# A transformer layer on one core: P times V in pairs, and the last transposes of P grouped with the first pair

## What is computed

```python
xn, ln = _ln(x, g_x, b_x), _ln(latents, g_l, b_l)
q = ln @ w_q
k, v = jnp.split(jnp.concatenate([xn, ln], axis=1) @ w_kv, 2, axis=-1)
sim = jnp.einsum('bhid,bhjd->bhij', q * scale, k)      # 64 x 576 a head
attn = jax.nn.softmax(sim, axis=-1)
out = jnp.einsum('bhij,bhjd->bhid', attn, v)
return _ln(out @ w_out, g_o, b_o)
```

## Time and profile before

| | before |
|---|---|
| profiled execution, us | 987.43 |
| its span, us | 985.6 |
| TensorE busy | 956.3 us, 97% |
| VectorE busy | 769.4 us, 78% |
| ScalarE busy | 440.2 us, 45% |
| GpSimd busy | 130.7 us, 13% |
| granted clock of TensorE | 1.00 |
| P times V, 1280 matmuls | 43.1 + 21.4 us |

### The profile page before, as it was taken

How to read it: one execution, slowest core, us unless ns; L and a number is a source line. 1 busy time by engine, 2 the same in 40 slices (tenths; PEclk the granted TensorE clock), 3 DMA queues, 4 the chain that set the end, 5 groups by cost and what they waited for, 6 DMA issues and landing times.

```text
span 985.6 us, 16666 instructions
## 1 busy us (share of the span) xinstructions
PE 956.3 (97%) x6400; PEld 778.0 (79%) x6400; DVE 769.4 (78%) x1647; ACT 440.2 (45%) x848; POOL 130.7 (13%) x145
## 2 busy tenths in 40 slices
PE   8999999999999999999999999999999999999997
PEld 7778788787888787887878888777676778888885
DVE  6547588789788888887887884578888598999985
ACT  4533664565366456546545653723333322222221
POOL 6420000101110101100111010023122000000000
PEclk9999999999999999999999999999999999999999
DMA  6688565866877684767758466081002950000000
GB/s 216 186 273 206 183 105 159 190 88 191 156 130 154 150 175 110 188 150 138 129 145 197 80 181 174 5 213 34 1 2 76 264 131 12 11 11 12 12 12 22
DMA packets 119451, 120.06 MB, mean 122 GB/s; under 512 B 47430, under 2 KB 88070, under 8 KB 117324
## 3 DMA queue, kind: packets, MB, share of 16 engines
q1 hardware_dynamic: 111980, 93.30, 35.5%
q0 software_dynamic: 6816, 24.64, 14.3%
q10 hardware_dynamic: 576, 1.05, 0.3%
HBM read 89.04 MB, written 29.93 MB: 121 GB/s over the span
## 4 chain that ended last, share of the span: by engine, by line
PE 53%; DVE 17%; DMA 12%; issue 7%; ACT 5%; SPq 4%; POOL 1%; DVEq 0%; ACTq 0%
PE ps_banks L147 13%; PE ps_banks L149 12%; PE ps_banks L148 12%; DMA scratch_rstd<-sb_rstd_b 7%; PE ps_banks L472 4%; SPq L132 4%; PE ps_banks L679 3%; DVE sb_kfull L915 2%; DVE sb_kT_lo L886 2%; PE ps_banks L746 2%; PE ps_banks L747 2%; PE ps_banks L748 2%; PE ps_banks L598 2%; DVE sb_b_stats L847 2%; DMA scratch_mean<-sb_a_mean_row 1%
## 5 line engine op out<-in xcount | busy, mean ns | idle before, releaser
L1442 ACT ACTIVATE sb_kT_hi<-sb_kfull 128x512 fp32r<-128x512 f32 x64 | 40.5, 632 | 161.2 <-DVE sb_kfull L915 161.2
L147 PE MATMUL ps_banks<-sb_zT_hi,sb_wkv_hi 128*128 128x512 f32 x256 | 106.1, 414 | 0.1
L149 PE MATMUL ps_banks<-sb_zT_hi,sb_wkv_lo 128*128 128x512 f32 x256 | 100.4, 392 | 0.0
L148 PE MATMUL ps_banks<-sb_wkv_lo,sb_zT_hi 128*128 128x512 f32 x256 | 100.3, 392 | 0.0
L147 PE MATMUL ps_banks<-sb_wkv_hi,sb_zT_hi 128*128 128x512 f32 x256 | 100.1, 391 | 0.0
L149 PE MATMUL ps_banks<-sb_wkv_hi,sb_zT_lo 128*128 128x512 f32 x256 | 100.0, 391 | 0.0
L148 PE MATMUL ps_banks<-sb_zT_lo,sb_wkv_hi 128*128 128x512 f32 x256 | 99.9, 390 | 0.0
L966 DVE CUSTOM_DVE_ANT_0 sb_probs<-ps_banks,sb_maskbias 128x576 f32<-128x576 f32 x64 | 48.1, 751 | 35.9 <-PE ps_banks L149 35.5
L147 PE MATMUL ps_banks<-sb_wgu,sb_z_hi 128*128 128x512 f32 (+1 forms) x192 | 73.7, 384 | 0.0
L148 PE MATMUL ps_banks<-sb_wgu,sb_z_hi 128*128 128x512 f32 (+1 forms) x192 | 72.1, 375 | 0.0
L149 PE MATMUL ps_banks<-sb_wgu,sb_z_lo 128*128 128x512 f32 (+1 forms) x192 | 71.9, 375 | 0.0
(11 more groups left out here) (268 smaller groups left out, 2419.0 us busy)
## 6 DMA issues: line engine op xcount, KB each, us to landing
sb_ctx<-in_ctx SPq DMA_DIRECT2D x16, 1024.0 KB
sb_ctxT<-in_ctx_t SPq DMA_DIRECT2D x16, 1024.0 KB, 8.3
scratch_wgu<-sb_w_both POOLq DMA_DIRECT2D x22, 512.0 KB
sb_wgu<-scratch_wgu SPq DMA_DIRECT2D x44, 256.0 KB, 4.7
sb_wdn<-scratch_wdn SPq DMA_DIRECT2D x8, 704.0 KB, 7.8
scratch_q<-sb_a_qk POOLq DMA_DIRECT2D x8, 512.0 KB, 6.2
sb_rstd_row<-scratch_rstd SPq DMA_DIRECT2D x16, 256.0 KB, 4.9
sb_qpack<-scratch_q SPq DMA_DIRECT2D x32, 128.0 KB, 8.5
```

The source lines that it names most:

```text
L147: e.matmul(o, wh, xh, start=i == 0, stop=False)
L148: e.matmul(o, wh, xl, start=False, stop=False)
L149: m = e.matmul(o, wl, xh, start=False, stop=i == n - 1)
L1442: e.activation(dst, src, ACT.Identity).then_inc(done)
```

## The change

TensorE: in the slots 0 to 3 P is now touched at two places. Slot 0 has K0 alone. Slot 1 turns P2 and P3, does P times V of the pairs 0 and 1, and then both lone transposes of P2 and P3, side by side in one bank; slot 3 does the pairs 2 and 3. In slots 6 and 7 nothing moves. ScalarE's copies follow, with one read-out signal for the two lone ones. The split of the last quarter of w_out moves from the end of batch 0 and slot 0 of batch 1 to slots 2 and 3 of batch 1.

```diff
             def transpose_p(b, n):
...
-                bank = claim(("pt", b, n))
-                e.transpose(psum[0:LQ, bank, 0:P], probs[j][:, chunk(b, CS)], ident[:, :]).then_inc(filled[bank])
+
+            def transpose_p_latents(b, *tiles):
+                bank = claim(("pt", b, tiles[0]))
+                for j, n in enumerate(tiles):
+                    took["pt", b, n] = took["pt", b, tiles[0]]
+                    on.wait_ge(p_normed, C * b + n + 1)
+                    m = e.transpose(psum[0:LQ, bank, j * P:(j + 1) * P], probs[n % 2][:, chunk(b, CS)], ident[:, :])
+                m.then_inc(filled[bank])
...
-                    if old and slot < 4:
-                        weigh_v(b - 1, slot)
-                    if old and slot < 2:
-                        transpose_p(b - 1, slot + 2)
+                    if old and slot == 1:
+                        transpose_p(b - 1, 2)
+                        transpose_p(b - 1, 3)
+                        weigh_v(b - 1, 0)
+                        weigh_v(b - 1, 1)
+                        transpose_p_latents(b - 1, 2, 3)
+                    if old and slot == 3:
+                        weigh_v(b - 1, 2)
+                        weigh_v(b - 1, 3)
                     if cur and slot >= 6:
                         transpose_p(b, slot - 6)
+                        transpose_p_latents(b, slot - 6)
...
-                    if b == 1 and slot == 0:
+                    if b == 1 and slot == 3:
                         lo_of_w_out(C - 1)
...
-                bank = taken(("pt", b, n))
-                copy(p_t[j][0:LQ, CS, :], psum[0:LQ, bank, 0:P], drained[bank])
+
+            def copy_p_latents(b, *tiles):
+                bank = taken(("pt", b, tiles[0]))
+                for j, n in enumerate(tiles):
+                    if C * b + n >= 2:
+                        on.wait_ge(v_weighed, C * b + n - 1)
+                    m = e.activation(p_t[n % 2][0:LQ, CS, :], psum[0:LQ, bank, j * P:(j + 1) * P], ACT.Copy)
+                m.then_inc(drained[bank])
...
-                    if old and slot < 2:
-                        copy_p(b - 1, slot + 2)
+                    if old and slot == 1:
+                        copy_p(b - 1, 2)
+                        copy_p(b - 1, 3)
+                        copy_p_latents(b - 1, 2, 3)
                     if cur and slot >= 6:
                         copy_p(b, slot - 6)
+                        copy_p_latents(b, slot - 6)
...
-                    if b == 0 and slot >= 4:
+                    if b == 0 and 4 <= slot < 7:
                         hi_of_w_out(slot - 4)
+                    if b == 1 and slot == 2:
+                        hi_of_w_out(C - 1)
```

## The result

The changed kernel took 1004.56 us (median of four runs, 999.98 to 1006.07) where the kernel before took 987.24 on the same chip (four runs, 984.4 to 989.51): ratio 1.0152, 95% interval 1.0128 to 1.0176. The forecast was 996, 985 to 1002. It went the way that was forecast, and nearly twice as far, so that it ended 2.6 us above the range.

A forecast was written before the change was run, and what follows sets the result against it. TensorE, 97% busy, was taken to just keep up with a loop through rstd's memory round trip. Odd batches +6.8, batch 1 +1.3, even +2.8, last -0.3 made 10.6; about 1.5 back left +9: 996 us, range 985 to 1002.

The forecast's parts named there:

- The mechanism: K1 waits for K0's own bank in even batches, for the turned weight's in odd batches 3 to 13; +9 us.
- the gain taken back: About 1.5 us subtracted from the sum, where an earlier K0 or a turn read out earlier helps.
- the last batch: Term of the sum for the final batch: -0.3 us.
- the wait for V: On TensorE, the first P times V no longer waits for the copy of V: 3.7 us saved.
- that for `tile_lo`: TensorE's later wait, up to 1.1 us, shrinks by what the scores came later.
- Laps to `sb_b_ve`: From K0 scaled to VectorE's last statistics: odd batches with a turn +6.8 us in all, even ones +2.8, batch 1 +1.3.
- The trip: Round trip of rstd through memory, from VectorE's last statistics to the next K0 scaled: still 18 to 19 us.
- What TensorE saves: Grouped P times V saves 0.6 us a batch, 9 to 10 over 15; with the V wait, 13 to 14 us.
- The first rival: TensorE's queue is the bound after all; if banks are free in time, 14 us come off: 973 us; chance 13%.
- The bound on the turn's bank: How much earlier the turned weight's bank is free with ScalarE's half in a shorter queue: 0 to 1.1 us, odd batches.
- It decides if K0 is scaled within 2.6 us of its end: Condition for the rival that TensorE's queue bounds the kernel: VectorE scales K0 before TensorE needs the bank for K1.
- The rule of the Trainium skill: Independent matmul groups should rotate through different PSUM banks; by it alone the change is a loss, with no number given.

The follow-up runs named there:

- the changed kernel again: The unaltered changed kernel run once more on the chip of the other experiments, as yardstick: ratio 1.0061 to the kernel before on the same chip.
- the freest order: Against the kernel before: P2 turned ahead of K0, P3 behind the first pair, both pairs, lone transposes behind K1; 0.9986, or 0.9937 with K scaled by a row always in SBUF.
- the kernel before without the row wait: The kernel before with K scaled by g_o, a row always in SBUF, so nothing waits for rstd's landing: ratio 0.9990 to the kernel before.
- the row always there: The changed kernel with K scaled by a row always in SBUF, spill and load of rstd kept: ratio 0.9987 to the kernel before.
- the kernel with y scaled later: The changed kernel with VectorE's two operations on y_row moved behind the scaling of K1 in odd batches: ratio 1.0210 to the kernel before.
- the first pair: The kernel before and the changed kernel as first measured, on one chip: 987.24 and 1004.56 us, ratio 1.0152.

## Why the prediction was half right

*The mechanism held, the size did not.* The steps that failed are terms of the sum: the gain taken back, the last batch, batch 0 and the clock at nothing. K1 starts 0.05 behind the weight's read-out in odd batches and 0.06 behind K0's scaling in even ones; the wait for V and that for `tile_lo` are gone, P times V is 4.3 us shorter (15 x 0.3 = 4.5 forecast). From K0 scaled to the first scores an even batch takes 10.3 (forecast 10.3) and an odd one with a turn, but for batch 3 with its dip of the clock, 11.55 to 11.8 (forecast 1.70 + 0.05 + 9.8). Laps to `sb_b_ve` grew by 7.4 in the odd batches without the dip of the clock (forecast 6.8, written for 6 x 1.1 = 6.6), 2.0 in the even ones (2.8), 1.7 in batch 1 (1.3): 11.1 for 10.9. The trip stayed at 18.5.

*What was mis-sized* is the rest of the sum, 9 forecast and 16.5 found:
- "I take about 1.5 back" did not come: 1.5. Every such gain lies inside the trip, which didn't shorten.
- the last batch, -0.3, was +1.0: 1.3. In turn 16 the transposes of P3 wait for its last scaling; some of it is the clock, at 0.91 in 640 to 660; the changed kernel again has the same wait of 3.0 there and 0.91 in 620 to 640.
- batch 0, +1.0, not foreseen; whether it is the moved w_out is not settled.
- the clock: 1.6 in batch 3, and 1.8 behind turn 16, of which the dip in the last stage is 1.6, in no term of mine. The first follows on a stand of TensorE of 1.7 us, which the new wait made; that it caused the dip is not shown, and nearly the same stand in the batches 7 and 9 had none behind it. The last can't be tied to the change: from its first matmul with `sb_wdn` to the end a kernel takes 177.2 to 177.3 us in 15 of the 20 profiles, the changed kernel again among them, and 178.8 in five.
The laps were 0.2 more. 0.2 + 1.5 + 1.3 + 1.0 + 3.4 = 7.4 of the 7.5 missing.

*"What TensorE saves"*, 13 to 14 us, is too large: the freest order without a row wait gave 7.3 in 14 laps, 0.52 a lap, where 0.6 and 3.7 for V were counted. The 0.6 was about right: with the waits named in these laps taken off both (3.3, and 1.7 in the kernel before without the row wait) it is 8.9, or 0.64 a lap. What failed are the waits. Of the V wait the kernel before without the row wait has only 2.5 left, and K0, now straight behind the last V, waits for `zT_lo` (3.8 in six places in the freest order, 7.2 in eight in the changed kernel), which I put at nothing. The first rival's 973 was out of reach for that reason too: it needed this saving whole.

*The bound on the turn's bank*, 0 to 1.1, is 0: with VectorE out of the way ScalarE's chain ends at the same time. I had named only VectorE.

*"It decides if K0 is scaled within 2.6 us of its end"* is borne out in kind: with the row always there the loss is gone. What I missed is how far the size hangs on the chip. The order ties TensorE to the landing, so 0.9 us more of trip costs the changed kernel 13 us of loop and the kernel before 6; a range from one chip's trip could not hold that. On the chips of the experiments the forecast of +9 would have been 3 too much.

The rule of the Trainium skill that the forecast cited (Perfetto Trace Analysis, "Matmuls": groups rotate through different banks) agrees with the runs in kind. They add a price: 5 us of loop come back when one unit less is claimed between K0 and K1 (the lone ones behind K1), and 2.0 us, with no gain in the time, when the unit taken away only moves ahead of K0 and the lone transposes take the tie over.

## What to carry to other kernels

When units take banks from one ring in claim order, write down for each claim which unit had its bank four claims ago and what ends that unit's read-out; an edit that only adds or drops one claim shifts every pair behind it, and may hand the tie to the next one. An engine that is 97% busy can still be only level with a loop through memory: price an order by how it ties that engine to the loop, and expect its cost to move with the chip. What a busy engine saves shows only when the other loops let it, so measure it once with those loops cut.

## What the runs showed of the hardware

- A spill of 2 KB in pieces of 4 bytes took 11 to 12 us, as a mean, from issue to the load back, on either queue (9.7 ahead of the large load), and ahead of 1 MB on the same queue it raised that load's landing from 5.1 to 13.9 us and the load back's from 5.0 to 7.8. Why the large one suffers was not tried.
- In the kernel with y scaled later, the uint16 operation of 128x512 on VectorE took 1.32 to 1.39 in the odd batches 3 to 13, against 0.43 in the changed kernel; beside each of the six ran an addition of GpSimd, as in batch 7:

```profile
336.15 1.65 POOL L1899 TENSOR_TENSOR sb_y_row<-sb_y_row,sb_b_o 128x512 f32<-128x512 f32 x1 [4.25 <-DVE sb_y_row L1003]
```

By the Trainium skill ("Trainium Architecture — The Big Picture", "What this means for kernel authors") VectorE and GpSimd contend for a shared pair of ports under an exclusive lock; the 1.39 agrees, and it is some 1 us of the 2.1 that the first maximum came later.
- The same program took 987.2 with the first pair and 979.3 to 980.8 on the four later chips, with 12.1 against 11.1 us from the spill of rstd to its load back, and the same change cost 1.5% and 0.6%. That the chip makes the difference is likely, not shown.
